# A mixture-of-experts stage that scatters with add: which scatters each scatter waits for

## The reference, cut to what matters

```python
def _L0_ffn_ref(x, Wg, bg, We, be, W1, b1, W2, b2):   # G=4 groups of E=8 experts, KG=2, KE=4
    ggates, gidx = _topk_gates(xf @ Wg + bg, KG)
    egates, eidx = _topk_gates(einsum('nd,gde->nge', xf, We) + be, KE)
    combine = gw[:, :, None] * ew                      # 8 of 32 experts for each node
    for g in range(G):
        h = gelu(einsum('nd,edm->enm', xf, W1[g]) + b1[g])     # 768 -> 384
        o = einsum('enm,emd->end', h, W2[g]) + b2[g]           # 384 -> 768
        y = y + einsum('end,ne->nd', o, combine[:, g, :])
x = x + ffn(layernorm(x))
```

## Time and profile before

| | |
|---|---|
| median of 3 runs | 1535.79 us (1532.27 to 1538.11) |
| the profiled execution | 1536.7 us |
| its span, first to last instruction | 1534.8 us |
| PE busy | 1361.7 us, 89% |
| DVE, ACT, POOL busy | 1158.5, 742.6, 502.0 us |
| tiles of experts, scatters | 91 copies of y (L2182), 92 scatters (L2045) |
| moved by DMA | 209 MB |

### The profile page before, as it was taken

One profiled execution on the slowest core, in us unless ns is written; L12 is line 12 of the kernel. 1 busy time (PEld: TensorE's weight loads), 2 busy tenths in 40 slices (PEclk: granted clock), 3 DMA queues, 4 the chain that ended last, 5 costly groups with the idle time before them and its releaser, 6 DMA issues. The chain is left out here.

```text
span 1534.8 us, 31149 instructions
## 1 busy us (share of the span) xinstructions
PE 1361.7 (89%) x7679; PEld 1134.6 (74%) x7690; DVE 1158.5 (75%) x1822; ACT 742.6 (48%) x1177; POOL 502.0 (33%) x556
## 2 busy tenths in 40 slices
PE   6888988878777879889975999999999999999995
PEld 3656656733232338889975999999999999999995
DVE  5479999899999987848877576555566655788882
ACT  3465565355556553412223455444455544666662
POOL 1000000002333320032324554555455555555563
PEclk9899999789999999999986999999999999999998
DMA  4300002041222214233466978766778876789963
GB/s 169 137 9 18 18 9 79 18 176 61 62 80 85 80 39 141 66 90 105 118 169 216 270 207 199 197 166 152 173 185 221 206 194 147 211 271 266 255 141 49
DMA packets 101471, 209.32 MB, mean 136 GB/s; under 512 B 19302, under 2 KB 58470, under 8 KB 101298
## 3 DMA queue, kind: packets, MB, share of 16 engines
q1 hardware_dynamic: 78402, 139.70, 27.7%
q0 software_dynamic: 22240, 66.69, 21.6%
q10 hardware_dynamic: 784, 2.36, 0.4%
HBM read 161.78 MB, written 54.93 MB: 141 GB/s over the span
## 5 line engine op out<-in xcount | busy, mean ns | idle before, releaser
L971 PE MATMUL ps_o<-prob,h_head 128*97 128x512 f32 (+1 forms) x480 | 188.3, 530 | 51.3 <-DVE prob L913 51.3
L2045 POOL DMA_INDIRECT out_nodes<-y,to_index x92 | 161.5, 1755 | 144.3 <-issue 89.1
L2346 PE MATMUL ps_h<-e_hi,e_xt_hi 128*128 (+1 forms) x546 | 193.1, 354 | 8.3 <-ACT e_xt_hi L2164 4.2
L971 PEld LDWEIGHTS ps_o<-prob,h_head 128*97 128x97 f32 x480 | 73.5, 165 | 165.6 <-issue 90.0
L2331 PE MATMUL ps_y<-e_hi,e_ht_hi 128*128 (+1 forms) x546 | 192.2, 352 | 3.6 <-DVE e_ht_lo L2263 2.2
L2346 PE MATMUL ps_h<-e_lo,e_xt_hi 128*128 (+1 forms) x546 | 185.2, 339 | 0.0
L2331 PE MATMUL ps_y<-e_hi,e_ht_lo 128*128 (+1 forms) x546 | 184.4, 338 | 0.0
L2331 PE MATMUL ps_y<-e_lo,e_ht_hi 128*128 (+1 forms) x546 | 184.2, 337 | 0.0
L2229 DVE TENSOR_TENSOR e_lo<-raw,e_hi (+1 forms) x189 | 175.9, 951 | 7.6 <-ACT e_hi L2172 6.7
L2182 ACT ACTIVATE y<-ps_y,gate 128x768 f32 (+1 forms) x91 | 82.2, 903 | 194.9 <-PE ps_y L2331 99.9
L805 ACT ACTIVATE score<-score,al_col 128x1250 f32<-128x1250 f32 x80 | 106.0, 1335 | 98.8 <-DVE score L856 98.8
(11 more groups left out here) (349 smaller groups left out, 3038.9 us busy)
## 6 DMA issues: line engine op xcount, KB each, us to landing
raw<-in_ew SPq DMA_DIRECT2D x192, 384.0 KB
w_room<-rel_dram SPq DMA_DIRECT2D x14, 640.0 KB, 4.4
b_all<-in_eb SPq DMA_DIRECT2D x32, 192.0 KB
al_src<-al_dram SPq DMA_DIRECT2D x1, 5000.0 KB, 14.9
xs<-in_x SPq DMA_DIRECT2D x5, 768.0 KB, 12.8
x_in_t<-in_x SPq DMA_DIRECT2D x10, 384.0 KB, 3.6
out_nodes<-x SPq DMA_DIRECT2D x10, 384.0 KB, 4.2
table<-xf SPq DMA_DIRECT2D x10, 384.0 KB, 2.7
```

The costliest lines, as they stand in the source:

```text
L971: turn = nc.tensor.matmul(ps_o[u][0:C1 + 1, c, 0:WID[c]], h_head[:, u, t, :], prob[:, t % 2, 512 * c:512 * c + WID[c]], start=(t == 0), st ...
L2045: nc.gpsimd.indirect_dma_start(out, bass.IndirectOffsetOnAxis(to_index[:, w:w + 1], 0), y[:, w, :], None, bounds_check=NP - 1, oob_is_err= ...
L2346: nc.tensor.matmul(ps_h[:, 0:HID], xt_hi[:, c, :], b[:, bass.ds(e % 2, 1), c * HID:(c + 1) * HID] .rearrange("p o m -> p (o m)"), start=(c ...
```

## The change

The table is gone, with everything that makes it and reads it. All scatters, and the bias add of the last block, signal one semaphore, `scattered`. Scatter k waits until that semaphore shows the bias add and all k scatters ahead of it, so that there is never a second scatter under way. The wait for a free buffer and the wait in `keep_y` are counts of the same semaphore. The bias add of block 8 signals `bias_added[0]` with the other even blocks, and the wait for these ahead of the loop now takes it in. The last scatter signals `scattered` as well. Beside this, the semaphore `gating_in` of ten loads at the start of `mix_and_route` is split in three, and each engine waits for what it reads: PE for `wr`, DVE for `br`, ACT for `b2`.

```diff
@@ mix_and_route: tensors
-        tile_row_i = sb("tile_row_i", [E, LIST], I32)
-        tile_row = sb("tile_row", [E, LIST])
-        any_row = sb("any_row", [1, LIST])
-        ended = sb("ended", [E, LIST], BF16)
-        ends = sb("ends", [E, 1])
@@ mix_and_route: semaphores
-        gating_in, b_row_in = sem("q_gating_in"), sem("q_b_row_in")
+        wr_in, br_in, b2_in, b_row_in = sem("q_wr_in"), sem("q_br_in"), sem("q_b2_in"), sem("q_b_row_in")
@@ mix_and_route: SyncE (the wg and we loads now signal wr_in, be and bg br_in, the three b2 loads b2_in)
-                sp.dma_start(wr[:, :, E:E + G], wg.rearrange("(k p) g -> p k g", p=P)).then_inc(gating_in, 16)
+                sp.dma_start(wr[:, :, E:E + G], wg.rearrange("(k p) g -> p k g", p=P)).then_inc(wr_in, 16)
...
@@ mix_and_route: GpSimd
-                nc.gpsimd.iota(tile_row_i[:, :], [[1, LIST]], base=-1, channel_multiplier=0).then_inc(consts, 1)
...
-                pool.wait_ge(consts, 19)
+                pool.wait_ge(consts, 18)
@@ mix_and_route: ScalarE
-                act.wait_ge(gating_in, 16 * (6 + G))
+                act.wait_ge(b2_in, 48)
@@ mix_and_route: VectorE
-                dve.wait_ge(consts, 19)
+                dve.wait_ge(consts, 18)
...
-                nc.vector.tensor_copy(tile_row[:, :], tile_row_i[:, :])
-                nc.vector.tensor_scalar(any_row[:, :], tile_row_i[0:1, :], 0.0, None, ALU.is_ge)
...
-                dve.wait_ge(gating_in, 16 * (6 + G))
+                dve.wait_ge(br_in, 32)
...
-                then(nc.vector.tensor_copy(ends[:, :], ps_sums[0:E, 2 * E:2 * E + 1]))
-                nc.vector.tensor_scalar(ended[:, :], tile_row[:, :], ends[:, :], None, ALU.is_ge).then_inc(tiles_made, 1)
...
-                dve.wait_ge(tiles_summed, 2)
-                nc.vector.tensor_tensor(s.before_row[:, :], ps_sums[0:1, P:P + LIST], any_row[:, :], ALU.add)
@@ mix_and_route: TensorE
-                        pe.wait_ge(gating_in, 16 * (6 + G))
+                        pe.wait_ge(wr_in, 16 * (1 + G))
...
-                nc.tensor.matmul(ps_sums[0:E, 2 * E:2 * E + 1], sum_up[:, 0:E], tiles_b[:, 0:1],
-                                 start=True, stop=False)
-                nc.tensor.matmul(ps_sums[0:E, 2 * E:2 * E + 1], sum_up[:, E:2 * E], tiles_b[:, 0:1],
-                                 start=False, stop=True)
...
-                pe.wait_ge(tiles_made, 2)
-                nc.tensor.matmul(ps_sums[0:1, P:P + LIST], tiles_b[:, 0:1], ended[:, :],
-                                 start=True, stop=True).then_inc(tiles_summed, 1)
@@ run_experts: GpSimd
-                def scatter(w, done):
+                def scatter(w):
...
-                                                 compute_op=ALU.add).then_inc(done, 16)
-
-                def load_before(k):
-
-                    before = pool.value_load(s.before_row[0:1, bass.ds(k, 1)], min_val=0, max_val=LIST)
-                    pool.reg_mov(even_done, 16 * ((before + 1) // 2) + 16)
-                    pool.reg_mov(odd_done, 16 * (before // 2) + 16)
-
-                def wait_before():
-
-                    even, odd = pool.snap(even_done), pool.snap(odd_done)
-                    pool.wait_ge(ready, 1)
-                    pool.wait_ge(scattered[0], even)
-                    pool.wait_ge(ready, 1)
-                    pool.wait_ge(scattered[1], odd)
+                                                 compute_op=ALU.add).then_inc(scattered, 16)
...
-                    pool.reg_mov(free, 16 * (k // 2) + 16)
+                    pool.reg_mov(free, 16 * k)
+                    pool.reg_mov(landed, 16 * k + 16)
...
-                    load_before(k)
...
-                    own = pool.snap(free)
+                    own, rest = pool.snap(free), pool.snap(landed)
                     pool.wait_ge(ready, 1)
-                    pool.wait_ge(scattered[u], own)
+                    pool.wait_ge(scattered, own)
                     next_to_index(k, u).then_inc(to_set, 1)
                     pool.wait_ge(ready, 1)
                     pool.wait_ge(to_set, after_x)
                     pool.wait_ge(y_made, next_x)
-                    wait_before()
-                    scatter(u, scattered[u])
+                    pool.wait_ge(scattered, rest)
+                    scatter(u)
...
-                for u in range(2):
-                    add_bias(NT - 2 + u, scattered[u])
+                add_bias(NT - 2, s.bias_added[0])
+                add_bias(NT - 1, scattered)
                 pool.wait_ge(third_kept, 2)
                 for u in range(2):
-                    pool.wait_ge(s.bias_added[u], 16 * (NT // 2 - 1))
+                    pool.wait_ge(s.bias_added[u], 16 * (NT // 2 - u))
...
-                wait_before()
-                scatter(2, last_scattered)
-                pool.wait_ge(last_scattered, 16)
-                pool.reg_mov(even_done, 16 * ((n + 1) // 2) + 16)
-                pool.reg_mov(odd_done, 16 * (n // 2) + 16)
-                wait_before()
+                pool.wait_ge(scattered, rest)
+                scatter(2)
+                pool.reg_mov(free, 16 * n + 32)
+                pool.wait_ge(scattered, pool.snap(free))
@@ run_experts: ScalarE, keep_y
-                    act.wait_ge(scattered[0], 16 * (k // 2) + 16)
-                    act.wait_ge(scattered[1], 16 * ((k + 1) // 2))
+                    act.wait_ge(scattered, 16 * k)
@@ program
-        s.before_row = sb("before_row", [1, LIST], I32, side="right")
...
-        s.scattered = [ctx.enter_context(nc.semaphore(f"scattered{u}")) for u in range(2)]
```

More of the change, by code:

```diff
@@ L1414, in _ @@
                 sp.wait_ge(filled, 2)
-                sp.dma_start(wr[:, :, E:E + G], wg.rearrange("(k p) g -> p k g", p=P)).then_inc(gating_in, 16)
+                sp.dma_start(wr[:, :, E:E + G], wg.rearrange("(k p) g -> p k g", p=P)).then_inc(wr_in, 16)
                 for g in range(G):
                     sp.dma_start(wr[:, :, g * EG:(g + 1) * EG],
-                                 we[g].rearrange("(k p) e -> p k e", p=P)).then_inc(gating_in, 16)
-                sp.dma_start(br[:, 0:E], be.broadcast_to([P, E])).then_inc(gating_in, 16)
-                sp.dma_start(br[:, E:E + G], bg.broadcast_to([P, G])).then_inc(gating_in, 16)
+                                 we[g].rearrange("(k p) e -> p k e", p=P)).then_inc(wr_in, 16)
+                sp.dma_start(br[:, 0:E], be.broadcast_to([P, E])).then_inc(br_in, 16)
+                sp.dma_start(br[:, E:E + G], bg.broadcast_to([P, G])).then_inc(br_in, 16)
                 for part in range(3):
-                    sp.dma_start(b2_raw[part * E:(part + 1) * E, :], b2).then_inc(gating_in, 16)
+                    sp.dma_start(b2_raw[part * E:(part + 1) * E, :], b2).then_inc(b2_in, 16)
                 def store_gates(t):
@@ L1946, in run_experts @@
             sem("gate_kept"), sem("index_set"), sem("first_set"), sem("to_set"), sem("h_ready"))
-        rows_kept, last_scattered = sem("rows_kept"), sem("last_scattered")
+        rows_kept = sem("rows_kept")
         third_made, third_listed, third_kept = sem("third_made"), sem("third_listed"), sem("third_kept")
@@ L2107, in _ @@
                 one_on, two_on = pool.alloc_register("one_on"), pool.alloc_register("two_on")
-                free = pool.alloc_register("free")
-                even_done, odd_done = pool.alloc_register("even_done"), pool.alloc_register("odd_done")
+                free, landed = pool.alloc_register("free"), pool.alloc_register("landed")
                 three_on, arrived = pool.alloc_register("three_on"), pool.alloc_register("arrived")
@@ L2144, in _ @@
                 pool.reg_mov(one_on, n + 1)
-                load_before(n)
-                to, made = pool.snap(two_on), pool.snap(one_on)
+                pool.reg_mov(landed, 16 * n + 16)
+                to, made, rest = pool.snap(two_on), pool.snap(one_on), pool.snap(landed)
                 next_to_index(n, 2).then_inc(to_set, 1)
@@ L2460, in program @@
         s.b1_in = ctx.enter_context(nc.semaphore("e_b1_in"))
-        s.gathered = ctx.enter_context(nc.semaphore("gathered"))
+        s.gathered, s.scattered = ctx.enter_context(nc.semaphore("gathered")), ctx.enter_context(nc.semaphore("scattered"))
         s.gathered_1 = ctx.enter_context(nc.semaphore("gathered_1"))
-        s.scattered = [ctx.enter_context(nc.semaphore(f"scattered{u}")) for u in range(2)]
         with ExitStack() as layer2:
```

## The result

| | before | after |
|---|---|---|
| median of 11 runs | 1534.61 us (1531.52 to 1538.11) | 1539.42 us (1534.78 to 1543.83) |
| ratio | | 1.0036, 95% interval 1.0024 to 1.0047 |
| the profiled execution, its span | 1534.8 us | 1538.9 us |
| PE, DVE, ACT, POOL busy | 1361.7, 1158.5, 742.6, 502.0 us | 1365.7, 1156.6, 743.2, 499.7 us |

The change costs 5.5 us (3.7 to 7.2). The forecast was 4.2 us and "no change by the 0.5% that can be told". The total fits, but by luck: terms were mis-sized by more than the total, in both directions, and nearly cancel.

What follows compares the result with a forecast made beforehand. PE was taken to bound the middle of the expert stage, but not its start, late stretch or end. Routing end and start +1.4, added wait +2.0, end +0.8 gave +4.2 on 1535.79: 1540.0 us, range 1532.5 to 1550.

Steps and rivals of the forecast that it cites:

- Setup: Start of mix_and_route: splitting the load semaphore in three gains 0, since ACT still needs the b2 rows, issued last.
- End of routing: End of the routing stage: DVE loses the comparison and the copy of `ends`, -0.5 us (bounds -0.6 and 0).
- Start of the expert stage: Ahead of POOL's register loads: waiting for block 8's bias add makes the first gate copy 2.3 us later; +1.4 net with routing.
- Lookup: POOL's table load and counts per tile: free in the middle, up to 0.5 us per tile back where POOL is late.
- The added wait: Each scatter waits for the one directly ahead; single late scatters mostly hidden: +2.0 us for the stage, bounds -3 and +14.
- POOL catches up 1.0 per tile: Expert stage: POOL can do a tile in 6.2 us, so it recovers 1.0 us per tile after a late scatter.
- The end: Last scatter: released by the landing ahead, +0.9 us, less 0.1 of register work: +0.8, bounds 0 and +2.
- A: Expert stage: the chain of scatters, landing plus 1.1 us per tile, becomes the bound; about +13, 1549 us; chance 0.22.
- PE idle in the middle windows: Sign in the later profile, middle of the expert stage, that would speak for A.
- B: The added wait never shows, as everything was in order already; only start and end remain: +2.2, 1538 us; chance 0.16.
- C: Relief: shorter POOL loop (-3.5 in the late stretch) and an early bias add (-1.3): about -4, 1532 us; chance 0.09.
- D: Start of the expert stage: transfers collide otherwise, gathers landing earlier or later: 1540 with 5 either way; chance 0.08.

Runs made afterwards that it cites:

- e_wait: The kernel before with only the wait counts changed, so every scatter waits for all scatters ahead, lookup kept: 1545.11 us, 1.0068.
- e_bias: The changed kernel with block 8's bias add awaited ahead of each scatter, not ahead of POOL's register loads: 1532.69 us, 0.9993.
- its pair: The same bias-add edit on the changed kernel with an unused tensor restoring the old addresses, with against without: worth 0.5 us (give or take 2.5).
- e_nolook: e_wait without the load of the table's entry in each tile; two semaphores and the making of the table stay: 1.0030, 4.6 us above the kernel before.
- e_again: The changed kernel timed once more, unedited, with a second trace: 1537.33 us, 1.0018 of the kernel before.
- e_both: The changed kernel with the edit of e_bias and an unused tensor that puts the old addresses back: 1535.15 us, 1.0008.
- the edit of `keep_rows`: VectorE's in_rows copy waits for its gather's landing, not POOL's gate copy: 1542.54 us (1.0052) on the changed kernel, 1540.05 us (1.0030) on the kernel before.

## Why the prediction was right or wrong

**Setup, 0.** Right. ACT still waits for the b2 rows, until 669.62 (669.36 in the earlier trace rows).

```profile
669.62 0.85 ACT L1563 ACTIVATE b_t<-b_raw 96x768 fp32r<-96x768 f32 x1 [9.23 <-DMA b_raw<-in_eb]
```

The first mix of PE ended about 1.5 us earlier than before, by TensorE's clock. Windows of before, then of e_wait, whose code there is that of before and which shows the same early rise:

```profile
660.00:670.00 10.00, 9.01 (x36) 9.01 (x37) 5.29 (x13) 1.22 (x2) 7.37 (x17) 0.66 0.60 138
```

```profile
660.00:670.00 10.00, 9.17 (x45) 9.17 (x46) 3.48 (x13) 0.48 (x2) 7.15 (x17) 0.83 0.58 127
```

PE was busy for 9.01 and 9.17 of these 10 us, and the granted clock rose from its level of 1.2 GHz to 2.4 GHz earlier in the one than in the other (means 0.66 and 0.83), with no edit between. It counts for no part of the change.

**End of routing, -0.5.** Right: 3.97 to 3.48 us ahead of the second index copy.

**Start of the expert stage, +1.9 without the part before.** Right. The landing was put at 8.5 us after its issue, and the loop's register loads start 8.9 us after it (822.58 to 831.44). Against the stage's start the loop's first gate copy is 2.6 us later than before (16.42 for 13.87), where 2.3 were forecast; the 0.4 us of slack behind it did not show, so this execution paid about 2.5 for the 1.9. e_bias and its pair give 3.8 and 0.5 us for taking the wait away.

**Lookup, free in the middle and at most 0.5 us a tile elsewhere, counted as 0.** The step that failed is the one that let relief lie outside the sum. It was weighed in the kernel before, where POOL has time to spare. With the wait in place 70 of 92 scatters stand until the landing ahead, and the lookup stands behind such a scatter and ahead of the gate copy and the gather that DVE waits for. e_nolook gives 5.8 us back (2.5 to 9.1) where the sum had nothing.

**The added wait, +2.0.** The mechanism was right, its price was not: alone it costs 10.4 us, near the upper bound of +14. A mis-sized step is "POOL catches up 1.0 per tile". It took the spacing of two scatters that did not wait for each other. With the wait the spacing is a landing plus 0.88 us. At 860 to 1200 us the median landing is 5.8, so an ordinary spacing is 6.7 and gives back 0.5 us, not 1.0. At 1200 to 1420 us it is 6.6 + 0.9 = 7.5 us, more than a plain tile, and half of the landings give nothing back. The 10.4 us are also the price with the lookup kept in, which the sum did not weigh together with the wait. The landings under load were put at 8.7 to 9.3 us; the longest is 9.3 us, as estimated. So it was their share and the recovery that were wrong, not their length.

The page "DMA: Bandwidth & Descriptors" of the Trainium skill (anatomy of a GpSimd-issued DMA), by whose fit an estimate of 2.9 us comes out and the wait would never show, is low by a factor of 2 here: the trace has 5.8 us at the median.

**The end, +0.8.** The scatter's part happened in the first trace and not in the second, and something else paid for it. POOL's timelines at the end, of after and of e_again:

```profile
1521.92 1.59 POOL L2026 DMA_INDIRECT out_nodes<-y,to_index  x1 [2.61 <-ACT y L2145]
...
1528.63 1.58 POOL L2026 DMA_INDIRECT out_nodes<-y,to_index  x1 [4.91 <-DMA out_nodes<-y,to_index]
```

```profile
1528.27 1.58 POOL L2026 DMA_INDIRECT out_nodes<-y,to_index  x1 [5.35 <-ACT y L2145]
```

In after the last scatter waits for the landing ahead and starts 2.06 us after y (1525.67 + 0.90), against 1.11 before: +0.95. In e_again it starts as soon as y lets it. From its start to the end of the span it is 10.3 us in after and 10.0 in e_again, against 11.4 before (1534.8 - 1523.44). The landing itself is no shorter (5.6 us in after, 5.7 before), so the old waits behind the last scatter cost about 1 us, where the sum had 0.1. Both effects together make the end -0.1 us in after and -1.5 in e_again, not +0.8.

**The sum.** Predicted: +1.4, 0, +2.0, +0.8. The runs, in steps: the wait alone +10.4 (e_wait); the lookup out -5.8 (e_nolook); one semaphore, the routing, the end and the bias add awaited at the scatters -3.4 (e_both); the start of the stage and the addresses +2.9 (the changed kernel's mean). Each step is uncertain by 2 to 3 us, and that they add up to 4.1 is arithmetic and no proof. But the total of 4.2 met it because a wait five times dearer met reliefs that had been left out, and that is luck.

**The rivals.** A (the chain of scatters is the bound) has the mechanism: most scatters do stand on the landing ahead, which it said and the forecast did not. Its price was +13 with the start and the end in it; e_wait, without these and with the lookup, lost 10.4, and the whole change 4.1. The sign that was named for it, PE idle in the middle windows, is not there (180.00 of 180 us busy). B is excluded by e_wait. C's relief exists, but inside the lost time, not instead of it. D is chance from run to run, and it exists ahead of the stage too: the routing stage's index copy of 0.18 or 1.55 us alone moves the end of that stage by 1.4 us.

## What to carry to other kernels

When a wait replaces a computed rule, cost the engine's queue as a chain under the new wait (landing plus issue, against the time of a tile) and not as single events covered by the old slack. Then cost again everything else on that queue, for instructions that were free beside an idle engine are not free in a chain. A tile of the engine that is the bound can keep its pace while the helper behind it has lost all its reserve; ask how many tiles stand between it and the first place where experts of one tile follow each other. And take an edit back to the kernel before it is called a cure: the edit of `keep_rows` cost the same there.

## What the runs showed of the hardware

- Moving tensors by the size of one row of 532 bytes changed a tile of 45 matmuls (18 for h, 18 for y, 9 transposes) from 7.24 to 7.27 us. Which tensor's address does it was not tried.
- A copy of 128 indices by POOL took 0.18 us or 1.55 us beside the same VectorE comparison. In the kernel before, that DVE operation ran from 813.83 for 1.49 us, and the copy from 813.81 to 815.36; in after it ran from 811.47, and the copy from 811.45 to 811.63. Rows of before, then of after:

```profile
813.83 1.49 DVE L1283 TENSOR_TENSOR one_row<-lanes,row_in_tile 128x1280 f16<-128x1280 bf16 x1
```

```profile
811.47 1.50 DVE L1283 TENSOR_TENSOR one_row<-lanes,row_in_tile 128x1280 f16<-128x1280 bf16 x1
```

  The page "SBUF — State Buffer" of the Trainium skill (section on who interferes with whom) has this rule: a VectorE instruction with two SBUF inputs and a GpSimd instruction that reads SBUF exclude each other for a whole instruction. The trace of before agrees: the copy ends when the other does, 0.04 us apart. In after the copy got through. The recorded starts are 0.02 us apart, copy first, in both, so they do not tell who will wait.
- POOL's small copies are drawn from about 1.04 us after a scatter's start on (1.03 and 1.08 in the rows above), inside its 1.58 us, with the rest of the scatter in their duration. So their mean duration grows when they queue behind scatters, and it also grows when they meet `in_rows` (0.61 us for 0.21).
- A scatter with add of 393 KB landed in 4.2 to 9.3 us (860 to 1420 us of after), and the next one started 0.88 us after the landing that let it go.
